# Other places for the steps of the first two attentions, integer rounding of weights, and a key spread on GpSimd

## The reference

```python
x = x + _L0_xattn_ref(_layernorm(x), ctx_1024, ctx_1024, Wq, bq, Wk, bk, Wv, bv, Wo, bo)
x = x + _L0_attn_ref(_layernorm(x), Wqkv, bqkv, Wout, bout, Wgate, bgate, pos_bias)
x = x + _L0_ffn_ref(_layernorm(x), w_gate, w_up, w_down)
# in both attentions, 16 heads of 16: softmax(q k / 4 + mask or bias) v, causal, then a projection;
# the second multiplies by a sigmoid gate ahead of its projection
def lpbq_dequant(w):                       # the weights of the FFN, in blocks of 32
    s = jnp.maximum(jnp.max(jnp.abs(wb), axis=-1, keepdims=True) / 7.0, 1e-12)
    wq = jnp.clip(jnp.round(wb / s), -8.0, 7.0) * s
```

## Time and profile before

| | |
|---|---|
| median of 3 runs | 1780.78 us (1777.43 to 1781.12) |
| the profiled execution | 1774.97 us |
| its span, first to last instruction | 1773.2 us |
| PE, DVE, ACT, POOL busy in the span | 87%, 46%, 32%, 28% |

### The profile page before, as it was taken

One profiled execution on the slowest core, in us unless ns is written; L12 is line 12 of the kernel. 1 busy time (PEld: TensorE's weight loads), 2 busy tenths in 40 slices (PEclk: granted clock), 3 DMA queues, 4 the chain that ended last, 5 costly groups with the idle time before them and its releaser, 6 DMA issues.

```text
span 1773.2 us, 30285 instructions
## 1 busy us (share of the span) xinstructions
PE 1539.7 (87%) x11788; PEld 978.6 (55%) x11788; DVE 823.6 (46%) x1636; ACT 567.8 (32%) x1409; POOL 489.8 (28%) x581
## 2 busy tenths in 40 slices
PE   4887777891899999999985777699999999999999
PEld 3766665440777777777763555444454454445445
DVE  3889998568645655555554777620011002001000
ACT  2444333577434445444540222220111111101110
POOL 2444332001024545454444888600000000000000
PEclk9999999996899999999996999999999999999999
DMA  7000000000012221111100000020000000000000
GB/s 260 20 9 2 1 0 1 1 0 24 14 48 84 65 83 42 36 42 36 41 13 1 1 1 0 17 103 0 0 12 0 0 0 12 0 0 12 0 0 12
DMA packets 18198, 43.99 MB, mean 25 GB/s; under 512 B 3040, under 2 KB 5600, under 8 KB 16992
## 3 DMA queue, kind: packets, MB, share of 16 engines
q1 hardware_dynamic: 18144, 43.24, 7.4%
HBM read 41.14 MB, written 2.10 MB: 24 GB/s over the span
## 4 chain that ended last, share of the span: by engine, by line
PE 70%; DVE 16%; issue 5%; POOL 4%; ACT 4%; DVEq 1%; DMA 0%; SPq 0%; POOLq 0%; ACTq 0%
PE ps L765 25%; PE ps L411 12%; PE ps L604 6%; PE ps L610 6%; PE ps L417 4%; PE ps L630 4%; PE ps L780 3%; PE ps L582 2%; PE ps L641 2%; POOL lrn L1595 1%; DVE amax L1231 1%; DVE R L1054 1%; DVE nmx L1101 1%; DVE R L1092 1%; DVE R L1169 1%
## 5 line engine op out<-in xcount | busy, mean ns | idle before, releaser
L765 PE MATMUL ps<-R 128*128 128x512 f32 x1024 | 440.6, 592 | 0.0
L765 PEld LDWEIGHTS ps<-R 128*128 128x128 f32 x1024 | 194.3, 190 | 243.5 <-issue 243.5
L411 PE MATMUL ps<-R 128*128 128x128 f32 (+1 forms) x1344 | 308.2, 389 | 7.8 <-DVE R L1227 3.5
L411 PEld LDWEIGHTS ps<-R 128*128 128x128 f32 x1344 | 192.0, 196 | 122.8 <-issue 114.3
L1465 DVE TENSOR_TENSOR R<-ps,w3s 128x256 f32<-128x256 f32 x16 | 6.8, 425 | 465.1 <-PE ps L780 465.1
L1555 POOL TENSOR_TENSOR R<-R,c_inv 128x1024 f32<-128x1024 f32 x64 | 122.4, 1912 | 243.7 <-DVE c_inv L1389 243.7
L963 ACT ACTIVATE R<-ps,c_nmx 128x257 f32<-128x257 f32 x256 | 118.3, 474 | 104.7 <-DVE c_nmx L1378 104.7
L1354 DVE COPY R<-ps 128x512 f32<-128x512 f32 x128 | 88.5, 692 | 128.5 <-PE ps L630 128.5
L610 PE MATMUL ps<-x_wv,R 128*128 128x256 f32 x512 | 132.1, 382 | 0.0
L604 PE MATMUL ps<-R,x_wk 128*128 128x256 f32 x512 | 125.3, 387 | 2.3 <-DVE R L1365 1.2
L604 PEld LDWEIGHTS ps<-R,x_wk 128*128 128x128 f32 x512 | 94.4, 192 | 21.5 <-issue 9.2
(11 more groups left out here) (178 smaller groups left out, 2297.6 us busy)
## 6 DMA issues: line engine op xcount, KB each, us to landing
R<-in_ctxT SPq DMA_DIRECT2D x64, 257.0 KB, 2.6
R<-in_f_h SPq DMA_DIRECT2D x4, 1024.0 KB, 5.1
R<-in_f_h SPq DMA_DIRECT2D x1, 4096.0 KB, 12.6
R<-in_f_w SPq DMA_DIRECT2D x3, 1024.0 KB, 5.4
R<-in_ctxk SPq DMA_DIRECT2D x16, 128.0 KB, 2.3
out<-x SPq DMA_DIRECT2D x4, 512.0 KB, 2.6
x<-in_x SPq DMA_DIRECT2D x1, 1792.0 KB, 8.3
R<-in_a_wqkv SPq DMA_DIRECT2D x1, 768.0 KB, 8.5
```

The source lines that it names most:

```text
L411: r = mm(dst, w[:, ki, fo * P:(fo + 1) * P], src[:, ki, :], start=(ki == 0), stop=(ki == KI - 1))
L765: r = mm(ps[:, ring[o % 4], :], w[:, k, o * P:(o + 1) * P], src[:, k, :], start=(k == 0), stop=(k == NF1 - 1))
```

## The change

Four things change, all of them in X0 and A0.

1. The slots of nearly all steps of all four engines. On PE all steps move by two slots, which leaves the order of its repeated group as it was. ACT takes the keys of a tile right behind its own `a_xnT`, and the values apart from them. DVE's order changes throughout; on POOL the bias in A0 comes late, on slot 15.
2. In A0 the keys are spread by POOL (`b_keys`, slot 6) and not by DVE; PE's scores wait for `k_spread`.
3. Dividing the weights writes 16-bit integers (`w_int`), which rounds them; multiplying reads these. The step `d_w_round` is gone: 12 instructions.
4. `d_scale` is a `scalar_tensor_tensor` with the factor as a broadcast second tensor, where it was a `tensor_scalar` with two per-partition scalars.

```diff
         W_PART = [P, 48 // NT, 32]
+        w_int = [sb(f"w_int{m}", W_PART, I16) for m in range(3)]
...
-                pe.wait_ge(s["k_masked"], tile(n, l))
+                if kind == A0:
+                    pe.wait_ge(s["k_spread"], tile(n - BASE[A0], l))
+                else:
+                    pe.wait_ge(s["k_masked"], tile(n if kind == X0 else n - NT, l))
...
-            steps_0 = [(2, p_turn), (4, p_project), (8, p_scores), (11, p_turn_probs), (13, p_values), (15, p_turn_out),
-                       (17, p_out)]
+                attention(X0, "x0", [(4, p_turn), (6, p_project), (10, p_scores), (12, p_turn_probs),
+                                    (15, p_values), (17, p_turn_out), (19, p_out)]),
...
-                attention(X0, [(3, a_xnT), (5, a_keys), (5, a_values), (10, a_exp), (12, a_pT), (16, a_oT)]),
-                attention(A0, [(3, a_xnT), (5, a_keys), (5, a_values), (5, a_gate), (10, a_exp), (12, a_pT)])])
+                attention(X0, [(3, a_xnT), (4, a_keys), (7, a_values), (10, a_exp), (12, a_pT), (16, a_oT)]),
+                attention(A0, [(3, a_xnT), (4, a_keys), (6, a_values), (8, a_gate), (10, a_exp), (12, a_pT)])])
...
-                v.tensor_scalar(xn[l], xl[:, i, l, :], mv[l][:, 0:1], rstd[l][:, :], ALU.subtract, ALU.mult)\
-                    .then_inc(s["xn_ready"], 1)
+                v.scalar_tensor_tensor(xn[l], xl[:, i, l, :], mv[l][:, 0:1], rstd[l][:, :].broadcast_to([P, D]),
+                                       ALU.subtract, ALU.mult).then_inc(s["xn_ready"], 1)
...
-                    v.tensor_tensor(w, w, wi.broadcast_to(W_PART), ALU.mult).then_inc(w_divided, 1)
-
-            def d_w_round(kind, m, i, n):
...
-                    v.tensor_scalar(w, w, MAGIC, None, ALU.add).then_inc(w_rounded, 1)
+                    v.tensor_tensor(w_int[m][:, :, :], w, wi.broadcast_to(W_PART), ALU.mult).then_inc(w_rounded, 1)
...
-                    v.scalar_tensor_tensor(w, w, -MAGIC, ws.broadcast_to(W_PART), ALU.add, ALU.mult)\
-                        .then_inc(wT_quant, 1)
+                    v.tensor_tensor(w, w_int[m][:, :, :], ws.broadcast_to(W_PART), ALU.mult).then_inc(wT_quant, 1)
...
+            def b_keys(kind, l, i):
+
+                pool.wait_ge(s["kT_copied"], KI * tile(i + BASE[kind], l))
+                k = kT[l].rearrange("p (c k) -> p c k", k=L).unsqueeze(2).broadcast_to([P, 8, 4, L])
+                m = mask_hr[:, :].unsqueeze(1).unsqueeze(3).broadcast_to([P, 8, 4, L])
+                p.tensor_tensor(kbd[l][:, 0:8 * P].rearrange("p (c h k) -> p c h k", h=4, k=L), k, m, ALU.mult)\
+                    .then_inc(s["k_spread"], 1)
...
-            run_lanes(pool, SLOTS0, [attention(kind, [(0, b_rsqrt), (2, b_bias), (7, b_values)]) for kind in (X0, A0)])
+                attention(X0, [(1, b_rsqrt), (3, b_bias), (9, b_values)]),
+                attention(A0, [(0, b_rsqrt), (6, b_keys), (10, b_values), (15, b_bias)])])
```

More of the change, by code:

```diff
@@ L229, in perceiver @@
         names = ("stats_ready mv_ready vare_ready rstd_ready xn_ready xnT_ready xnT_copied x_biased "
-                 "qk_ready v_ready k_masked qT_copied v_copied v_turned v_spread scores_ready scores_masked max_ready scores_shifted "
+                 "qk_ready v_ready k_masked k_spread qT_copied v_copied v_turned v_spread scores_ready scores_masked max_ready scores_shifted "
                  "probs_ready sum_ready pT_ready pT_copied o_ready o_normed oT_ready oT_copied oT_gated "
@@ L259, in link @@
             eng.wait_ge(chain, links[chain])
-        w_max, w_scale, w_inverse, w_divided, w_rounded = map(
-            sem, ("w_max", "w_scale", "w_inverse", "w_divided", "w_rounded"))
+        w_max, w_scale, w_inverse, w_rounded = map(sem, ("w_max", "w_scale", "w_inverse", "w_rounded"))
         wT_quant, wT_turned, wT_copied = sem("wT_quant"), sem("wT_turned"), sem("wT_copied")
@@ L534, in attention @@
                          for at, step in steps])
-            steps_0 = [(2, p_turn), (4, p_project), (8, p_scores), (11, p_turn_probs), (13, p_values), (15, p_turn_out),
-                       (17, p_out)]
-            run_lanes(pe, SLOTS0, [attention(X0, "x0", steps_0), attention(A0, "a0", steps_0)])
+            run_lanes(pe, SLOTS0, [
+                attention(X0, "x0", [(4, p_turn), (6, p_project), (10, p_scores), (12, p_turn_probs),
+                                    (15, p_values), (17, p_turn_out), (19, p_out)]),
+                attention(A0, "a0", [(4, p_turn), (6, p_project), (10, p_scores), (12, p_turn_probs),
+                                    (15, p_values), (17, p_turn_out), (19, p_out)])])
             for l in range(NL):
@@ L1162, in d_w_divide @@
                     dve.wait_ge(w_inverse, 3 * i + m + 1)
-                    v.tensor_tensor(w, w, wi.broadcast_to(W_PART), ALU.mult).then_inc(w_divided, 1)
-            def d_w_round(kind, m, i, n):
-                if m < 3:
-                    w, wm, ws, wi = w_part(m, i)
-                    dve.wait_ge(w_divided, 3 * i + m + 1)
-                    v.tensor_scalar(w, w, MAGIC, None, ALU.add).then_inc(w_rounded, 1)
+                    v.tensor_tensor(w_int[m][:, :, :], w, wi.broadcast_to(W_PART), ALU.mult).then_inc(w_rounded, 1)
             def d_w_multiply(kind, m, i, n):
@@ L1207, in _ @@
             run_lanes(dve, SLOTS0, [
[L1208 to L1214, removed]
+                attention(X0, [(0, d_norm), (1, d_scale), (6, d_keys), (8, d_turn_values), (9, d_mask),
+                               (10, d_max), (10, d_shift), (12, d_sums), (13, d_norm_out), (18, d_add)]),
+                attention(A0, [(0, d_norm), (0, d_w_max), (1, d_scale), (2, d_w_scale), (4, d_w_inverse),
+                               (7, d_w_divide), (7, d_turn_values), (8, d_mask), (9, d_max), (10, d_shift),
+                               (12, d_sums), (13, d_norm_out), (16, d_w_multiply), (16, d_gate_out), (18, d_add),
+                               (19, d_f_stats)], enter_a0)])
             def scales(i0, i1, done):
@@ L1514, in b_values @@
                     .then_inc(s["v_spread"], 1)
-            run_lanes(pool, SLOTS0, [attention(kind, [(0, b_rsqrt), (2, b_bias), (7, b_values)]) for kind in (X0, A0)])
+            run_lanes(pool, SLOTS0, [
+                attention(X0, [(1, b_rsqrt), (3, b_bias), (9, b_values)]),
+                attention(A0, [(0, b_rsqrt), (6, b_keys), (10, b_values), (15, b_bias)])])
             pool.wait_ge(f0_mv, T)
```

## The result

| | before | after |
|---|---|---|
| median (range), 4 runs each | 1780.95 us (1777.43 to 1782.12) | 1767.7 us (1766.2 to 1768.07) |
| ratio, 95% interval | | 0.9927 (0.991 to 0.9944) |
| the profiled execution, its span | 1774.97 us, 1773.2 us | 1768.07 us, 1766.3 us |
| X0, a tile (masks, 15 distances) | 7.40 us | 7.74 us |
| A0, a tile | 9.81 us | 8.37 us |

What follows compares the result with a forecast made beforehand. It took DVE to bound A0 and a chain across the engines to bound X0. A0's -15.2 and X0's +2.3 gave -12.9 us: 1762 us for the profiled execution, 1768 us with 5.8 for the median; range 1732 to 1781 us.

Steps and rivals of the forecast that it cites:

- DVE bounds A0, and 2.6 us a tile leave its list: A0: DVE is full; rounding (2.0 us in three tiles of four) and key spread (1.08 us) leave its list.
- The pair that excludes each other: DVE instructions with two SBUF inputs, or a `tensor_scalar` within SBUF, and POOL's run one after the other, first starter first.
- `d_scale` losing the race in every tile: A0: POOL's key spread starts first and holds `d_scale`, about 2.2 us; 2.2 us of waiting come into each tile.
- A0's 8.8 us a tile: A0's mean period after the change, from 9.81 us; over 15 distances a gain of 15 us.
- my 8.97: A0: summed chain of a tile with weights, in us; tiles without weights were put at 8.19.
- X0's +2.3 us: X0: shift and POOL's small sum and power are held, so 15 distances lose 0.15 us each.
- my 7.47: X0: summed chain of a tile after the change, in us, against 7.32 before.
- my 2.95: X0: the chain's first step, up to the next statistics, in us.
- the first two rivals: X0 at 6.7 us: only A0 held, 1756 us, chance 0.14; or nothing held, A0 at 7.57, 1738 us, chance 0.22.
- Nothing counted for the clock: A0: PE's clock expected at its upper level after the change, counted as no gain, as DVE sets the pace.
- the 5.8 us that I added for the median: Whole kernel: the median of the runs stood 5.8 us above the profiled execution, so 1762 became 1768 us.
- -12.9 forecast: A0 and X0 together: -15.2 us in A0 and +2.3 us in X0.

Runs made afterwards that it cites:

- e1: Kernel before with the integer rounding alone, the twelve rounding instructions gone and all places as before; 1776.95 us, A0 9.51 us a tile.
- e4: Kernel after with `d_scale` as the `tensor_scalar` of before; 1760.99 us, X0 7.68 and A0 8.25 us a tile.
- e5: Kernel after with DVE's X0 list reordered: sums and reciprocal ahead of the key spread, transposition of values right behind `d_scale`; 1770.87 us, X0 8.09 us a tile.
- e13: Kernel after with A0's key spread on DVE, `d_scale` as `tensor_scalar`, and only statistics and norm_out ahead of `d_scale` in DVE's X0 list; 1745.59 us.
- e8: Kernel after with A0's key spread taken from POOL and put back on DVE; 1762.25 us, A0 8.13 us a tile.
- e2: Kernel after with POOL in A0 waiting for `d_scale` before the key spread, and the weights' divide ahead of `d_scale` on DVE; 1763.49 us, A0 8.05.
- e3: Kernel after with the tables of before for X0 on all four engines, and PE's for A0; 1765.65 us, X0 7.55 us a tile.
- e12: Kernel after with A0's key spread on DVE, `d_scale` as `tensor_scalar`, and X0's orders of before on all engines; 1757.13 us, X0 7.45, A0 8.03.

## Why the prediction was right, step by step

- *DVE bounds A0, and 2.6 us a tile leave its list.* Right, but the rounding alone was worth 0.3 us a tile in e1, 0.7 in a round that the clock did not spoil, and not the 2.0 that it shows: its 2.05 was mostly waiting for POOL, and the wait passed to the divide and the small scale. The trace of before has the free length: the last rounding, at 296.02, started 0.15 us ahead of the value spread and took 0.32. The prediction had said that the mean was "this and nothing else", and still counted the full 2.0 as leaving; the order made that come true, since divide and small scale now run free, 0.49 and 0.13 us, the divide ahead of the transposition that releases POOL.
- *The pair that excludes each other, and `d_scale` losing the race in every tile.* Right, in place and size: 1.85 to 2.11 us in 15 of 16 tiles, and PE's turn idle for it. That the form would be held "since it reads two tensors" is only half of it: e4 has the `tensor_scalar` held in the same place for 1.98 us. The turn went to the waiting DVE as in the earlier trace rows. The Trainium skill, page "SBUF — State Buffer", section "Who interferes with whom", says that a DVE instruction with two SBUF inputs contends with a GpSimd instruction that reads SBUF, and by it the new form is held; the trace agrees, 2.11 us against 0.48, though the second tensor is one broadcast column.
- *A0's 8.8 us a tile.* The term was 0.43 too high. In the tile from 184.15 to 192.63 us, 8.48 against my 8.97: the spread took 1.89 and not 1.97 (0.08), the power was not held (0.24; over all tiles its mean is 0.65, so 0.08 and not 0.18 of a mean tile), divide to add took 0.81 and not 0.89, and the other ten steps are each within 0.03, 0.09 together.
- *X0's +2.3 us.* Right in its sign and in both holds, 2.8 us short. A steady tile takes 7.59 us, every fourth 7.8, on the mean 7.65 against my 7.47. Two steps failed. From the key spread to `d_scale` it is 1.99 us (94.29 to 96.28) and not 1.88, since key spread, small sum and power come to a little more than in the rows of before. And where the list said 0.33 from add to norm_out, the trace has 0.39, and 0.62 in every fourth tile, where norm_out waits 0.27 for PE's values. These stand behind PE's turn, which waits 0.71 us for `d_scale`, late for the held sum and power. The chain was added up on DVE alone, without that way back through PE. The transposition to the statistics was 0.07 shorter than my 2.95, which hid a part of it.
- *"X0 goes to some 6.7 us" if the holds are away* (the first two rivals). Wrong: e5 has them away and stands at 8.09. The holds were beside a loop through PE and ACT. The prediction had named a chain across the engines for the kernel before and then let it go. e13, which shortens the loop, gets 6.98.
- *Nothing counted for the clock.* In A0 it rose from 0.91 to 1.00 in the second part, as expected, but it was worth something: before, DVE waited 1.4 us a round for PE at 0.92, 2.7 us in all, and after the change 0.2. That is some 2.5 of A0's 21.6 us, which "DVE sets the pace" had at nothing. At the FFN's start the clock is lower (0.72 against 1.00) and 3.3 us are lost in the pair, but e1 loses 2.8 with the old places.
- *The third attention.* Step missed: `d_scale` is also called in A1, 16 times, so the new form can cost there too, 0 to 2.6 us at the same clock.
- *Sum.* By the profiled pair the stages give -21.6 in A0, +5.1 in X0, +0.2 for fill and passages, +3.3 in the FFN, +4.1 in A1 and +2.0 elsewhere: -6.9 us. By the medians it is -13.3; the profiled execution of before was one of its fastest, 6 us under its median. The profile of e1, which ran near its median, hints where these 6 us lie: against before its FFN is 2.8 us longer, A1 1.6 and A0's drain (last mask to first `f_mv`) 1.5, and e1 changes nothing there. So most of the +9.6 us that the pair shows outside A0 and X0 is before's fast profile, and the 5.8 us that I added for the median stood for it. By the medians, A0 and X0 come to -16.5 against -12.9 forecast, and some +3 is left for the rest, A1's form most likely among it. A0 gained 6.4 us more than forecast, X0 lost 2.8 more, and the rest lost 3 that were not counted. That the total fits to 0.3 us is luck: these errors cancelled.

## What to carry to other kernels

When two engines shut each other out, a busy share says nothing: read durations against the free one of the same shape, and before removing a slow instruction ask which one will stand in its place beside the other engine. Work moved from the full engine to its partner of this kind buys nothing if the partner then holds the instruction that starts the next tile (e8: back on the full engine it was 0.24 us a tile faster). And a hold is only worth removing where it lies in the loop: e5 removed two and lost 0.35 us a tile, e13 left one on an instruction that nobody awaits, shortened the loop and gained 0.65.

## What the runs showed of the hardware

- The hold strikes very small instructions too: POOL's sum of one column a row went from 0.22 to 1.04 us beside DVE's key spread, and a DVE `tensor_scalar` of 12 columns from 0.13 to 0.97 beside POOL's key spread (e2).
- A held DVE instruction of 256 columns ends 0.14 us (`tensor_scalar` in the earlier trace rows) to 0.28 us (`scalar_tensor_tensor`) behind POOL's: it keeps part of its own length.
- A `scalar_tensor_tensor` whose second tensor is a broadcast column takes 0.48 us free (after), the `tensor_scalar` with two such columns 0.41 in the same place (e4). In X0's old order the two are 0.44 (e3) and 0.37 (before).
- POOL's value spread in X0 takes 1.97 us in the old order and 1.89 in the new one, with the same operands (first e12, then after). In the old order it starts 0.16 us into a free `d_scale`; in the one tile of before where it started ahead of `d_scale`, at 146.68, it took 1.90. So the 0.08 us look like waiting for the rest of `d_scale`; no run tested it.

```profile
L1512 POOL TENSOR_TENSOR R<-R,mask x16: 1966/1968/1969, 29.6 to 140.2; 128x1024 f32<-128x1024 f32 x16
```

```profile
L1515 POOL TENSOR_TENSOR R<-R,mask x15: 1892/1893/1894, 29.6 to 137.0; 128x1024 f32<-128x1024 f32 x15
```
